# A two-layer decoder: the last mixture of experts on tokens sorted by expert, its routing spread over the next batch

## Chip, cores and metric

The kernel runs on one core of a Trainium2 chip. The time is the device time in microseconds (us) of one execution, inputs and outputs in the chip's memory; what stands below is the median of several runs, and the lowest and highest beside it. One further execution was taken by the profiler.

## What is computed

Four sequences of 512 tokens with 128 features pass two decoder layers. The first has an attention (A), a cross attention (B) and a mixture of 8 experts (C); the second an attention with relative positions (D), a cross attention to 154 context tokens (E), a causal attention with 16 heads (F), and a mixture of experts (G). The change concerns G, which is this, on all 2048 tokens at once:

```python
logits = xf @ router_w + router_b
vals, idx = top_k(logits, 2)
scores = softmax(vals)
cap = int(floor(n * 0.125))                         # 256 of 2048
oh = one_hot(idx, 8)
pos = cumsum(cumsum(oh, axis=0), axis=1)            # over tokens, then over the two choices
emask = oh * (pos < cap)
tmask = sum(emask, axis=-1)
m = max(einsum('tke,e->tk', emask, arange(8)), axis=-1)   # the one expert of a token
def ff(w1e, w2e, w3e):                              # 128 -> 256 -> 128
    return gelu(xf @ w2e * (xf @ w1e)) @ w3e
y = vmap(ff)(w1, w2, w3)[m, arange(n)]
slot = where(tmask[..., None] > 0, y[:, None, :], xf[:, None, :])
out = einsum('tkD,tk->tD', slot, scores)            # added to the residual
```

Each token needs the output of one expert only, `m`, and how many tokens came before it decides which, so the count runs on from batch to batch.

## The kernel before

Tokens lie in tiles of 128, four to a batch (`NT`). Every engine has a program of its own, written out stage by stage, with semaphores between them: `pe_` for TensorE (PE), `act_` for ScalarE, `dve_` for VectorE (DVE), `pool_` for GpSimd (POOL), `sp_` for the queue that issues DMAs. The order of the calls in these programs is the order of the work on that engine; an engine waits where its program waits. `ch(...)` in VectorE's program is a chain: the next instruction waits until this one has ended.

The first layer is written out batch by batch. Its mixture C runs once for all batches on sorted tokens. `dve_C_choose` finds each token's expert, `pe_C_rank` (L666 to L671) and `dve_C_slot` (L679 to L689) give it a row in a buffer in memory, `pool_C_send` (L696) scatters the tokens there by four indirect DMAs a batch. After the last batch a table says for each of 23 tiles (`NS`, 16 tiles and 7 for experts' unfilled ends) which rows and which expert it has (L762 to L780). Then a loop over the 23 tiles, six of them loaded ahead (`NXB`): `flip` transposes one (L709), `hidden` multiplies it with the first weights, which POOL has copied into place (L718, L833), ScalarE does the Gelu (L753), `result` multiplies with the second weights (L729), L798 puts the output into SBUF and the queue stores it to the same rows. Sixteen gathers (L837) bring the rows back in the tokens' order.

The second layer is a hardware loop over the batches (`Fori`), on every engine: the projection of D (`pe_D1`: context of E, bias L320, projection L315), E (`pe_X` and its partners), F, and G. Where the loop turns, VectorE adds the residual (L327) and normalizes it (`dve_norm`), and PE transposes the result (L263) as soon as that is there; until then it runs matmuls without a use (L259). In E the row maxima (L565) follow the scores (L450), and the reciprocals (L575) follow the last of the values (L493). In F the key projections (L1344) are rotated by VectorE (L1489 to L1491), the queries by VectorE (L1501) and added by POOL (L1543).

G before is in `pe_G`, `act_G` and `dve_G`. It is dense: for each of the 8 experts all 512 tokens of the batch go through both hidden matmuls (L1569, L1573, two chunks of 128 features each), ScalarE copies one product out (L1612), VectorE multiplies the two (L1644), ScalarE does the Gelu (L1626), PE multiplies with the third weights (L1599), and VectorE adds what belongs to the expert under a mask (L1700):

```python
ins = V.scalar_tensor_tensor(o, ps[:, 6 + e % 2, i * P:(i + 1) * P],
                             sel[:, i, e:e + 1], x[:, i, :], ALU.mult, ALU.add)
```

The router lies inside this work: gate matmuls (L1560), logits (L1649), the two choices (L611 to L618, twice), the counting matmuls (L1582 to L1587), and the pick of expert and scale (L1659 to L1690). In each turn PE goes on to the next batch only after the last expert.

## Time and profile before

| what | before |
|---|---|
| median of 3 runs | 1775.34 us (1773.99 to 1780.18) |
| profiled execution | 1777.35 us, its span 1775.5 us |
| TensorE (PE) busy | 1538.5 us, 87% |
| VectorE (DVE) busy | 1028.7 us, 58% |
| ScalarE (ACT) busy | 822.4 us, 46% |
| GpSimd (POOL) busy | 192.6 us, 11% |
| mean granted TensorE clock | 0.94 of full |
| share of the chain that ended last | PE 75%, DVE 12%, issue 6%, ACT 2%, SPq 2% |

The span reaches from the first to the last instruction; the time of the execution holds a little more. Busy time of PE counts matmuls of float32, which appear as two records each, and also matmuls without a use. "Issue" in the chain is time in which the engine waited for nothing that the profile shows. The stages lie, in us from the span's start: A and B to 310, C to about 405, D to about 897, and then the loop over E, F and G, with a turn at about 1115, 1333 and 1557.

### The profile page before, as it was taken

What the parts mean: (1) busy time and instruction counts of PE and PEld (TensorE: products, weight loads), DVE (VectorE), ACT (ScalarE), POOL (GpSimd) and SP (SyncE); (2) the same over time, 40 slices, a digit from 0 to 9 for tenths busy, and PEclk for the clock granted to TensorE, in tenths of its full rate; (3) what the DMA queues carried; (4) which work ended last, traced back from release to release, by engine and by line L of the source; (5) the groups of instructions that cost most, each with busy time, mean ns of one, the idle gap of its engine ahead of it and who ended that gap; (6) DMA issues with size and microseconds to landing.
All of it is one profiled execution on the core that took longest, in us unless ns stands there. A gap on an engine that the chain in (4) does not pass through costs nothing.

```text
span 1775.5 us, 46299 instructions
## 1 busy us (share of the span) xinstructions
PE 1538.5 (87%) x18075; PEld 936.6 (53%) x18110; DVE 1028.7 (58%) x2616; ACT 822.4 (46%) x2030; POOL 192.6 (11%) x147
## 2 busy tenths in 40 slices
PE   3988888666399999999779999889998899988998
PEld 2343443663267666666433665346663466534665
DVE  4364553326477777777535765467653666547655
ACT  1313223331266666666422774327643276442764
POOL 1010110234120020200002000020000200002000
PEclk9989989787699999999879999999998999999999
DMA  9500000112230100000030000000000000000000
GB/s 332 226 16 1 16 7 1 40 50 85 60 131 4 35 8 23 19 13 5 16 98 1 2 2 1 12 1 2 2 1 11 1 2 2 1 8 1 2 2 6
DMA packets 54165, 55.25 MB, mean 31 GB/s; under 512 B 26673, under 2 KB 39857, under 8 KB 52785
## 3 DMA queue, kind: packets, MB, share of 16 engines
q1 hardware_dynamic: 52912, 50.05, 8.8%
q8 instruction: 150, 2.46, 0.6%
q0 software_dynamic: 1024, 2.10, 0.4%
q14 instruction: 79, 0.64, 0.1%
HBM read 30.18 MB, written 21.95 MB: 29 GB/s over the span
## 4 chain that ended last, share of the span: by engine, by line
PE 75%; DVE 12%; issue 6%; ACT 2%; SPq 2%; DMA 1%; POOL 0%; ACTq 0%; DVEq 0%; POOLq 0%
PE ps L1002 7%; PE ps L1374 5%; PE ps L1393 5%; PE ps L493 4%; PE ps L982 4%; PE ps L1407 4%; PE ps L992 4%; PE ps L1020 4%; PE ps L1599 3%; PE ps L259 3%; PE ps L1362 3%; DVE arena L565 3%; PE ps L1573 3%; PE ps L1569 3%; PE ps L467 3%
## 5 line engine op out<-in xcount | busy, mean ns | idle before, releaser
L1132 DVE TENSOR_REDUCE nmax<-ps 128x1 f32<-128x512 f32 x256 | 166.8, 684 | 60.7 <-PE ps L992 59.9
L1450 ACT ACTIVATE arena<-ps,arena 128x512 f32<-128x512 f32 (+3 forms) x256 | 135.4, 531 | 117.5 <-DVE arena L1508 109.8
L1508 DVE TENSOR_REDUCE arena<-ps 128x1 f32<-128x512 f32 (+3 forms) x256 | 124.3, 487 | 76.2 <-PE ps L1378 74.1
L1092 ACT ACTIVATE arena<-ps,nmax 128x512 f32<-128x512 f32 x172 | 119.0, 692 | 85.4 <-DVE nmax L1132 84.4
L1393 PE MATMUL ps<-sqc,arena 128*128 128x128 f32 x640 | 108.1, 288 | 20.5 <-DVE arena L1516 19.5
L565 DVE TENSOR_REDUCE arena<-ps 128x8 f32<-128x1232 f32 x64 | 89.2, 1438 | 40.6 <-PE ps L455 40.1
L1140 DVE COPY arena<-ps 128x512 f32<-128x512 f32 x128 | 88.0, 688 | 36.9 <-PE ps L1002 35.4
L575 DVE RECIPROCAL arena<-ps 128x128 f32<-128x128 f32 x8 | 7.7, 959 | 170.0 <-PE ps L493 170.0
L1516 DVE TENSOR_SCALAR arena<-arena 128x512 f32<-128x512 f32 (+3 forms) x256 | 100.8, 394 | 9.1
L1374 PE MATMUL ps<-arena 64*128 64x384 f32 (+3 forms) x512 | 105.2, 489 | 0.0
L259 PE MATMUL ps<-sel,identb 128*128 128x512 bf16 x385 | 100.9, 417 | 3.3 <-issue 2.6
L1407 PE MATMUL ps<-arena 128*64 128x128 f32 x1280 | 98.2, 284 | 0.0
L1002 PE MATMUL ps<-sqc,arena 128*128 128x128 f32 x688 | 95.6, 282 | 2.9 <-issue 1.7
L1461 ACT COPY arena<-ps 128x512 f32<-128x512 f32 (+3 forms) x256 | 96.1, 430 | 3.1 <-PE ps L1393 3.0
L1393 PEld LDWEIGHTS ps<-sqc,arena 128*128 128x128 f32 x640 | 71.4, 141 | 48.5 <-DVE arena L1516 31.4
L1002 PEld LDWEIGHTS ps<-sqc,arena 128*128 128x128 f32 x688 | 74.8, 143 | 22.3 <-issue 17.4
L306 ACT ACTIVATE root<-var 128x4 f32<-128x4 f32 x32 | 6.6, 206 | 158.8 <-DVE var L288 138.5
L1100 ACT COPY arena<-ps 128x512 f32<-128x512 f32 x128 | 74.4, 581 | 11.6 <-PE ps L1002 11.5
L1644 DVE TENSOR_TENSOR arena<-ps,arena 128x512 f32<-128x512 f32 x64 | 43.9, 691 | 58.6 <-PE ps L1573 46.5
L992 PEld LDWEIGHTS ps<-rk,cw 64*128 64x128 f32 x512 | 44.4, 192 | 60.7 <-issue 56.0
L595 POOL TENSOR_TENSOR arena<-arena,m 128x640 f32<-128x640 f32 x8 | 10.0, 1255 | 612.2 <-ACT arena L526 612.2
L992 PE MATMUL ps<-rk,cw 64*128 64x168 f32 (+25 forms) x512 | 75.3, 414 | 0.0
(332 smaller groups left out, 3062.2 us busy)
## 6 DMA issues: line engine op xcount, KB each, us to landing
xs_d<-onehot SPq DMA_DIRECT2D x3, 3072.0 KB, 31.1
cw<-in_cw SPq DMA_DIRECT2D x2, 2048.0 KB, 13.0
rv<-in_rv SPq DMA_DIRECT2D x2, 1536.0 KB, 19.4
late<-in_gw SPq DMA_DIRECT2D x3, 1024.0 KB, 10.5
xs_d<-onehot SPq DMA_DIRECT2D x1, 2560.0 KB, 22.5
onehot<-q_s SPq DMA_DIRECT2D x96, 8.0 KB
arena<-xs_d SPq DMA_DIRECT2D x23, 64.0 KB, 1.8
xs_d<-arena SPq DMA_DIRECT2D x23, 64.0 KB, 1.6
```

The lines of the kernel that those rows point to most:

```text
L259: nc.tensor.matmul(ps[:, FILL[k][1], :], identb[:, :], sel[:, 0:4, :].rearrange("p a n -> p (a n)"), start=True, stop=True)
L565: nc.vector.tensor_reduce(top_x[:, i, :, 2 * hp:2 * hp + 2], ps[:, bank:bank + NG4, 0:2 * KP].rearrange("p g (h k) -> p g h k", h=2)[:, :, ...
L992: nc.tensor.matmul(ps[:, (4 * Q + j) % 5, k0:k1], AI[b % 2][64 * z:64 * z + 64, par * NW + w, :], rk[64 * z:64 * z + 64, r0:r0 + k1 - k0], ...
L1002: ins = nc.tensor.transpose(ps[:, TB[j % 2], i * P:(i + 1) * P], PB[k % 6][:, i * P:(i + 1) * P], c["ident"])
L1092: nc.scalar.activation(PB[k % 6], ps[:, k % 5, :], ACT.Exp, bias=nmax[:, u:u + 1], accum_out=rsum[:, b % 2, u:u + 1]).then_inc(SD["exp"], 1)
L1132: nc.vector.tensor_reduce(nmax[:, k % NU:k % NU + 1], ps[:, k % 5, :], AX.X, ALU.max, negate=True)\
L1374: nc.tensor.matmul(ps[:, FSB[n % 2][h], 0:wd], TF["q%d" % a][HALVES[h], i * P:(i + 1) * P], TF["kr%d" % (a % 2)][HALVES[h], 0:wd], start=T ...
L1393: ins = nc.tensor.transpose(ps[:, FTB[h], j * P:(j + 1) * P], TF["p%d" % (n % 2)][:, h * S + j * P:h * S + (j + 1) * P], c["ident"])
L1407: ins = nc.tensor.matmul(ps[HALVES[h], 4, i * P:(i + 1) * P], TF["v"][:, v0:v0 + KD], PTF[n % 2][h][:, j * P:(j + 1) * P], start=(j == 0), ...
L1450: nc.scalar.activation(TF["p%d" % (n % 2)][:, h * S:h * S + wd], ps[:, FSB[n % 2][h], 0:wd], ACT.Exp, bias=TF["nmax"][:, k4:k4 + 1], accum ...
L1508: nc.vector.tensor_reduce(TF["nmax"][:, k4:k4 + 1], ps[:, FSB[n % 2][h], 0:wd], AX.X, ALU.max, negate=True)\
L1516: nc.vector.tensor_scalar(TF["p%d" % (n % 2)][:, h * S:h * S + wd], TF["p%d" % (n % 2)][:, h * S:h * S + wd], TF["rinv"][:, k4], None, ALU ...
```

## The change

G works on sorted tokens as C does, and its parts move. The loop over the batches is written out on every engine. After F of a batch only the gate and the two choices follow (`pe_G_gate`, `dve_G_gate`). The rest of the routing of batch b stands in the next batch: the counting matmuls ahead of the scores of E, the copy of their result ahead of the first row maximum, the second score's exponential in `act_X`, the pick of the expert ahead of the reciprocals, the ranking matmuls behind the values, the slot in F behind its second norm, the four scatters on POOL ahead of F's rotary additions. After the last batch its routing runs too, then the table, the loop over 23 tiles and 16 gathers. In this loop a tile takes eight hidden records, four result records and one transpose, one ScalarE copy, one product, one Gelu and one copy out of PSUM. POOL copies both hidden weights of the expert together. B and E share their semaphores, so every wait in E counts on from B (`both`); table building is shared between C and G (`dve_tiles`).

```diff
--- before.py
+++ after.py
@@ pe_X
+            if k == "E" and b:
+                pe_G_count(pe, b - 1)
             for n in range(NXH):
+                if k == "E" and b and n == 1:
+                    pe.wait_ge(SG["seen"], b)
                 scores(n)
...
                 values(j)
+            if k == "E" and b:
+                pe_G_rank(pe, b - 1)
             pe_bias(DH[k][0], 1, k + "_bo")
@@ act_X
+            if k == "E" and b:
+                act_G_second(act, b - 1)
@@ dve_X
             dve_norm(dve, ch, b, k, src=y)
+            if k == "E" and b:
+                dve_G_seen(dve, b - 1)
...
             nc.vector.tensor_tensor(low, top_x, high, ALU.subtract).then_inc(s["mt"], 1)
+            if k == "E" and b:
+                dve_G_pick(dve, ch, b - 1)
+            dve.wait_ge(s["pv"], both(k, b) * NPER + NPER)
@@ pe_F
+            if b:
+                pe.wait_ge(SG["slot"], b)
             for i in range(NT):
                 ins = nc.tensor.matmul(ps[:, 5 + i // 2, i % 2 * 256:i % 2 * 256 + 256], xnT[:, i * P:(i + 1) * P],
                                        fwv[:, :], start=True, stop=True)
@@ dve_F
             dve_rms(dve, ch, b, 2, xn[:, :, :], yn, row["F_g1"])
+            if b:
+                dve_G_slot(dve, ch, b - 1)
@@ G
+        def act_G_second(act, b):
+            act.wait_ge(SG["d"], b + 1)
+            nc.scalar.activation(gs["e2"][:, :], gs["t1"][:, :], ACT.Exp).then_inc(SG["e2"], 1)
...
+        def pe_G_rank(pe, b):
+            pe.wait_ge(SG["pick"], b + 1)
+            if b:
+                pe.wait_ge(SG["slot"], b)
...
+        def pool_G_send(pool, b):
+            pool.wait_ge(SG["slot"], b + 1)
+            for n in range(NT):
+                nc.gpsimd.indirect_dma_start(xs_d, bass.IndirectOffsetOnAxis(ap=slot4[:, b * NT + n:b * NT + n + 1], axis=0),
+                                             yn4(b)[:, n, :], None).then_inc(SC["sent"], 16)
+
+        def pe_G(pe):
+            pe.wait_ge(SG["slot"], B)
+            nc.tensor.matmul(ps[:, 0, 0:E2], c["ones"], carry[:, :], start=True, stop=True).then_inc(SG["count"], 1)
+            pe.wait_ge(SG["table"], 1)
...
+            def hidden(s):
+                e = nc.tensor.value_load(expert4[0:1, s:s + 1], min_val=0, max_val=E2 - 1)
+                pe.wait_ge(SC["w1"], NS + s + 1)
+                pe.wait_ge(SC["xt"], NS + s + 1)
+                if s >= 2:
+                    pe.wait_ge(SG["p"], s - 1)
+                for j in range(2 * NC2):
+                    ins = nc.tensor.matmul(ps[:, 2 + j // NC2 + 2 * (s % 2), j % NC2 * P:j % NC2 * P + P],
+                                           TG[f"w{s % 2}"][:, j * P:(j + 1) * P], TG[f"xT{s % 2}"], start=True, stop=True)
+                ins.then_inc(SC["h"], 1)
+                return e
+
+            def result(s, e):
+                pe.wait_ge(SC["hs"], NS * NC1 + s + 1)
+                if s >= 2:
+                    pe.wait_ge(SC["yb"], NS + s - 1)
+                for j in range(NC2):
+                    ins = nc.tensor.matmul(ps[:, 6 + s % 2, 0:P], TG[f"h{s % 2}"][:, j * P:(j + 1) * P],
+                                           gw3[:, bass.ds(e * NC2 + j, 1), :].rearrange("p o n -> p (o n)"),
+                                           start=(j == 0), stop=(j == NC2 - 1))
+                ins.then_inc(SC["y"], 1)
+
+            flip(0)
+            flip(1)
+            e = hidden(0)
+            for s in range(NS):
+                if s + 2 < NS:
+                    flip(s + 2)
+                following = hidden(s + 1) if s + 1 < NS else None
+                result(s, e)
+                e = following
+
+        def act_G(act):
+            nc.scalar.activation(warm[:, 19:20], c["ones"][:, 0:1], ACT.Gelu)
+
+            def linear(s):
+                act.wait_ge(SC["h"], NS + s + 1)
+                if s >= 2:
+                    act.wait_ge(SG["p"], s - 1)
+                nc.scalar.copy(TG[f"a{s % 2}"], ps[:, 3 + 2 * (s % 2), 0:HID2]).then_inc(SG["a"], 1)
+
+            linear(0)
+            for s in range(NS):
+                if s + 1 < NS:
+                    linear(s + 1)
+                act.wait_ge(SG["p"], s + 1)
+                if s >= 2:
+                    act.wait_ge(SC["y"], NS + s - 1)
+                nc.scalar.activation(TG[f"h{s % 2}"], TG[f"p{s % 2}"], ACT.Gelu).then_inc(SC["hs"], 1)
+
+        def dve_G(dve, ch):
...
+            def product(s):
+                dve.wait_ge(SC["h"], NS + s + 1)
+                if s >= 2:
+                    dve.wait_ge(SC["hs"], NS * NC1 + s - 1)
+                dve.wait_ge(SG["a"], s + 1)
+                V.tensor_tensor(TG[f"p{s % 2}"], ps[:, 2 + 2 * (s % 2), 0:HID2], TG[f"a{s % 2}"], ALU.mult).then_inc(SG["p"], 1)
...
+            for s in range(NS):
+                if s + 2 < NS:
+                    copy(s + 2)
+                if s + 1 < NS:
+                    product(s + 1)
+                dve.wait_ge(SC["y"], NS + s + 1)
+                if s >= 4:
+                    dve.wait_ge(SC_st[s % 4], 16 * (st_c[s % 4] + s // 4))
+                V.tensor_copy(TG[f"y{s % 4}"], ps[:, 6 + s % 2, 0:P]).then_inc(SC["yb"], 1)
+            for b in range(B):
+                dve.wait_ge(SC_yg[b], 2 * 16 * NT)
...
+            for z in range(4):
+                pool.wait_ge(SC_st[z], 16 * 2 * st_c[z])
+            for n in range(NTT):
+                nc.gpsimd.indirect_dma_start(yg4(n // NT)[:, n % NT, :], None, xs_d,
+                                             bass.IndirectOffsetOnAxis(ap=slot4[:, n:n + 1], axis=0)).then_inc(SC_yg[n // NT], 16)
@@ the program of TensorE
-            with pe.Fori(0, B) as b:
+            for b in range(B):
                 pe_D1(pe, b)
...
+                pe_X(pe, b, "E")
+                pe_F(pe, b)
+                pe_G_gate(pe, b)
+            pe_G_count(pe, B - 1)
+            pe_G_rank(pe, B - 1)
+            pe_G(pe)
@@ the program of GpSimd
+            for b in range(B):
                 pool_D1(pool, b)
...
+                pool_X(pool, b, "E")
+                if b:
+                    pool_G_send(pool, b - 1)
+                pool_F(pool, b)
+            pool_G_send(pool, B - 1)
+            pool_G(pool)
```

## Rows read from the trace of the kernel before

**Rows 1.** the chain of waits, 1140 to the end: start, us, what

```profile
1285.46 1.06 PE ps L1560 x8
...
1306.91 1.78 PE ps L1599 x16
...
1340.23 1.11 PE ps L263 x4
...
1725.68 1.06 PE ps L1560 x8
```

**Rows 2.** timeline, VectorE at the end: start, us, what [idle before]

```profile
1771.69 1.13 DVE L1700 SCALAR_TENSOR_TENSOR rv<-ps,gt_sel,x 128x128 f32 x4 [0.73 <-PE ps L1599]
```

**Rows 3.** timeline, the turn from the second batch to the third

```profile
1333.32 0.53 PE L426 MATMUL ps<-ctxT,sqw 128*128 128x160 f32 x2 [1.96 <-issue]
...
1335.79 0.82 DVE L552 TENSOR_TENSOR arena<-ps,rowb 128x640 f32<-128x640 f32 x1 [3.20 <-PE ps L429]
...
1335.95 1.16 PE L315 MATMUL ps<-sqw,aoT 128*128 128x128 f32 x8
...
1337.27 0.76 DVE L327 TENSOR_TENSOR x<-ps,rv 128x256 f32<-128x256 f32 x2 [0.65 <-PE ps L315]
```

**Rows 4.** timeline, the router inside G, second batch

```profile
1290.70 0.18 DVE L1649 TENSOR_TENSOR gt_logit<-ps,rowb 128x32 f32<-128x32 f32 x1
...
1293.24 0.19 DVE L618 TENSOR_TENSOR arena<-gt_eq,gs_top 128x32 f32<-128x32 f32 x1
...
1293.98 0.79 PE L1587 MATMUL ps<-arena,sqc 128*128 128x48 f32 x6
...
1297.20 0.16 DVE L1659 TENSOR_SCALAR gs_t<-gs_e 128x4 f32<-128x4 f32 x1
...
1300.33 0.16 DVE L1687 TENSOR_TENSOR gs_cz<-gs_m 128x4 f32<-128x4 f32 x1
```

**Rows 5.** timeline, VectorE at the end of cross attention

```profile
1379.99 0.96 DVE L575 RECIPROCAL arena<-ps 128x128 f32<-128x128 f32 x1 [22.79 <-PE ps L493]
```

**Rows 6.** timeline, first layer, from the last choice to the first tile

```profile
317.41 0.41 PE L666 MATMUL ps<-oh,sqc 128*128 128x32 f32 x2 [1.47 <-DVE oh L618]
...
319.69 0.17 DVE L689 CAST slot<-gs_top 128x4 int32<-128x4 f32 x1
...
327.30 6.32 SPq L816 DMA_DIRECT2D arena<-xs_d  x6
...
329.28 0.45 PE L709 MATMUL ps<-sqc,arena 128*128 128x128 f32 x1 [8.77 <-DMA arena<-xs_d]
```

**Rows 7.** timeline, first layer, from the last tile through the gathers

```profile
383.53 0.29 DVE L798 TENSOR_TENSOR arena<-ps,arena 128x128 f32<-128x128 f32 x1 [1.41 <-PE ps L729]
...
387.25 1.00 POOL L837 DMA_INDIRECT late<-xs_d,slot  x1 [9.53 <-DMA xs_d<-arena]
...
406.21 0.94 POOL L837 DMA_INDIRECT late<-xs_d,slot  x1 [0.30 <-issue]
```

**Rows 8.** timeline of POOL, first rotary addition of the third batch

```profile
1401.19 1.27 POOL L1543 TENSOR_TENSOR arena<-arena 128x512 f32<-128x512 f32 x1 [62.95 <-DVE arena L1501]
```

**Rows 9.** timeline, first layer's tile loop, first hidden and last transpose

```profile
331.16 2.05 PE L718 MATMUL ps<-arena 128*128 128x128 f32 x8 [0.49 <-DVE arena L787]
...
377.66 0.27 PE L709 MATMUL ps<-sqc,arena 128*128 128x128 f32 x1
```

**Rows 10.** groups by form, ScalarE: what, count, busy us, mean ns, idle before

```profile
L1461 ACT COPY arena<-ps 128x256 f32<-128x256 f32 x64 | 20.7, 374 | 2.5 <-PE ps L1393 2.5
...
L1626 ACT ACTIVATE arena<-arena 128x512 f32<-128x512 f32 x64 | 40.4, 631 | 13.1 <-DVE arena L1644 13.1
```

**Rows 11.** DMA issues of the page: tiles, op, count, us to landing

```profile
late<-xs_d,slot POOLq DMA_INDIRECT x16, 2.5
```

**Rows 12.** windows: stretch, us, busy of each engine, PE clock, DMA share

```profile
360.00:365.00 5.00, 3.29 (x19) 2.94 (x19) 0.58 (x2) 1.57 (x7) 0.92 (x2) 0.79 0.24 66
...
1341.00:1345.00 4.00, 2.46 (x14) 0.98 (x14) 0.00 (x0) 1.38 (x3) 0.00 (x0) 1.00 0.00 0
```

More of the change, by code:

```diff
@@ L445, in scores @@
                 if n >= 2:
-                    pe.wait_ge(s["top"], b * NXH + n - 1)
+                    pe.wait_ge(s["top"], both(k, b) * NXH + n - 1)
                 k0 = 0 if k == "B" else min(i * P, KS)
@@ L1544, in pool_F @@
                     .then_inc(SF["qr"], 1)
-        SG = {n: sem("s_g_" + n) for n in ("gate", "d", "e2", "oh", "cum", "h", "a", "p", "hs", "y", "acc")}
+        SG = {n: sem("s_g_" + n) for n in ("gate", "d", "e2", "oh", "cum", "seen", "pick", "rank", "slot", "count", "table", "a", "p")}
+        ld_c, st_c = ([len(range(z, NS, n)) for z in range(n)] for n in (NXB, 4))
+        NC2 = HID2 // P
         used[0] = 0
-        TG = dict(**{n + str(i): cut(S) for n in ("a", "p") for i in range(2)}, h0=cut(2 * S), h1=cut(2 * S),
-                  oh=cut(NT * 2 * E2), sum=cut(2 * E2))
@@ L1629, in dve_G, with dve_G_seen, dve_G_pick @@
-        def dve_G(dve, ch, b):
+        def dve_G_seen(dve, b):
+            dve.wait_ge(SG["cum"], b + 1)
+            nc.vector.tensor_copy(TG["cum"], ps[:, 7, 64:64 + NT * CE]).then_inc(SG["seen"], 1)
+        def dve_G_pick(dve, ch, b):
             V = nc.vector
-            dve_rms(dve, ch, b, 3, xn[:, :, :], yn, row["F_g2"])
-            ch(nc.vector.tensor_tensor(x[:, :, :], x[:, :, :], xn[:, :, :], ALU.add))
-            dve.wait_ge(SG["gate"], b + 1)
-            lg, oh1, oh2, pos, junk, sel = (gt[n][:, :, :] for n in ("logit", "oh1", "oh2", "pos", "junk", "sel"))
+            lg, oh1, oh2, pos, junk = (gt[n][:, :, :] for n in ("logit", "oh1", "oh2", "pos", "junk"))
@@ new lines, in dve_G, with copy @@
+        def dve_G(dve, ch):
+            V = nc.vector
+            dve.wait_ge(SG["count"], 1)
+            dve_tiles(ch, SG["table"])
+            def copy(s):
+                dve.wait_ge(SC["tx"], NS + s + 1)
+                if s >= 2:
+                    dve.wait_ge(SC["h"], NS + s - 1)
+                V.tensor_copy(TG[f"xT{s % 2}"], ps[:, s % 2, 0:P]).then_inc(SC["xt"], 1)
+            def product(s):
+                dve.wait_ge(SC["h"], NS + s + 1)
+                if s >= 2:
+                    dve.wait_ge(SC["hs"], NS * NC1 + s - 1)
+                dve.wait_ge(SG["a"], s + 1)
+                V.tensor_tensor(TG[f"p{s % 2}"], ps[:, 2 + 2 * (s % 2), 0:HID2], TG[f"a{s % 2}"], ALU.mult).then_inc(SG["p"], 1)
+            copy(0)
+            copy(1)
+            product(0)
+            for s in range(NS):
[9 more added lines that the diff above has]
+                dve.wait_ge(SC_yg[b], 2 * 16 * NT)
+                for i in range(NT):
+                    ins = V.scalar_tensor_tensor(xo4(b)[:, i, :], yg4(b)[:, i, :], cy4[:, b * NT + i:b * NT + i + 1], xo4(b)[:, i, :],
+                                                 ALU.mult, ALU.add)
+                ins.then_inc(s_xout, 1)
@@ new lines, in sp_G, with load @@
+        def sp_G(sp):
+            sp.wait_ge(SC["sent"], 2 * 16 * NTT)
+            sp.wait_ge(SG["table"], 1)
+            def load(s):
+                r = sp.value_load(rows4[0:1, s:s + 1], min_val=0, max_val=XROWS - P)
+                if s >= NXB:
+                    sp.wait_ge(SC["tx"], NS + s - NXB + 1)
+                sp.dma_start(XBG[s % NXB], xs_d[bass.ds(r, P), :]).then_inc(SC_ld[s % NXB], 16)
+            for s in range(NXB):
+                load(s)
+            for s in range(NS):
+                r = sp.value_load(rows4[0:1, s:s + 1], min_val=0, max_val=XROWS - P)
+                sp.wait_ge(SC["yb"], NS + s + 1)
+                sp.dma_start(xs_d[bass.ds(r, P), :], TG[f"y{s % 4}"]).then_inc(SC_st[s % 4], 16)
+                if s + NXB < NS:
+                    load(s + NXB)
@@ L1919, in _ @@
             dve.wait_ge(s_const[4], 16 * (len(GROUPS[4]) + 1))
-            ch = Chain(dve, SH[1]["ch"], CH[last])
-            with dve.Fori(0, B) as b:
-                ch.turn(b)
+            ch = Chain(dve, SH[1]["ch"], 0)
+            ch.turn(0)
+            for b in range(B):
                 dve_D1(dve, ch, b)
-                if "E" in stages:
-                    dve_X(dve, ch, b, "E")
-                if "F" in stages:
-                    dve_F(dve, ch, b)
-                if "G" in stages:
-                    dve_G(dve, ch, b)
-                if last != "G":
-                    nc.vector.tensor_copy(tmp[:, 0:1], x[:, 0, 0:1]).then_inc(s_xout, 1)
-                ch.end()
+                dve_X(dve, ch, b, "E")
+                dve_F(dve, ch, b)
+                dve_G_gate(dve, ch, b)
+            dve_G_seen(dve, B - 1)
+            dve_G_pick(dve, ch, B - 1)
+            dve_G_slot(dve, ch, B - 1)
+            dve_G(dve, ch)
         @block.gpsimd
```

267 lines of the change are left out of this document (119 added, 148 removed).

## Prediction, made before the changed kernel ran

> **What bounds the kernel now.** I read the chain of waits first, over the second layer only, to see which engine carries it, then the timeline at one turn of the batch loop, then the same views over the first layer's mixture of experts, which already runs on sorted tokens and so has rows for nearly everything that the change adds.
>
> The second layer is a loop over four batches, and the tensor engine (PE) carries it: the chain in there is made of pieces such as 16 expert matmuls in 1.78 us, 0.111 us each [rows 1]. In each turn the last mixture (G) runs all 8 experts over all 512 tokens. The stretch from the start of the gate's matmuls (L1560) to the first transpose of the next batch's cross attention (L263) holds the rest of G, the loop's turn, and the next batch's residual and norm. In the second turn it is 1285.46 to 1340.23, 54.77 us [rows 1]; the other two turns repeat the pattern with 54.85 and 56.16, together 165.8. After the last gate, which starts at 1725.68, the kernel has 49.8 us left to its end at 1775.5 [rows 1, 2]. What the change gains and pays lies in these four stretches, and in what it inserts into cross attention (E) and attention (F).
>
> **Part 1, the three turns between batches.** The dense experts and the turn of the loop go. Between gate and transpose there stays: the gate's matmuls, 1.06, so they end at 1286.5. PE goes on with context, bias and projection, which last from 1333.32 to 1337.11, 3.8 us, so to 1290.3 [rows 3]. DVE takes the logits through both top choices, L1649 at 1290.70 to the end of the last L618 at 1293.43, 2.73 us [rows 4], now from 1286.65 to 1289.4; then L552, 0.82, to 1290.3; then residual and norm, 2.96 from L327 (1337.27) to L263 (1340.23) [rows 1, 3]. The two engines come to the residual together, so this chain has no slack. The transposes start at about 1293.4, 7.9 us after the gate's start; three turns cost 23.8 where 165.8 stood: minus 142.0.
>
> **Part 2, what is inserted in the next batch.** The counting matmuls stand ahead of the first scores, where PE has just waited for q_t, and nothing covers them: L618 ends at 1293.43 and L1587 at 1294.77, 1.3 us [rows 4], three times: plus 3.9. PE's wait on "seen" comes behind the first scores, which cover DVE's copy of 64 columns. Who waits there is DVE's row of maxima, and it is late by the same 1.3, not more. The pick goes where DVE sits idle for 22.79 us ahead of L575 [rows 5]: L1659 at 1297.20 to L1687 at 1300.33, with one step more and one copy less 3.3 us [rows 4], and four updates of x: hidden, and 4.5 a turn if it weren't. The ranking matmuls stand behind the values, while PE waits for those reciprocals: nothing, at most their 1.3. The slot chain runs in F before L1489, where DVE waits for the key projections: nothing, at most its 1.0; ranking and slot together are 2.45 (L666 at 317.41 to the end of L689 at 319.86 [rows 6]). PE's wait on the slot comes after the key projections, when the slot has long been there. On POOL four sends stand ahead of the rotary additions. I price a send by the pace of layer 0's gathers, 15 steps from 387.25 to 406.21, 1.26 each [rows 7], 5.0 in all. They start at about 1393.7 and end at 1398.8; POOL's first addition now starts at 1401.19 [rows 8], so the margin is 2.4 us. Behind POOL stand DVE's rotation of the third pair and then PE's queries.
>
> **Part 3, the new tail**, on the clock of the old kernel. The last gate ends at 1726.74. Choice with its handover 2.85, to 1729.6; counting 1.35; copy 0.3; the pick up to the one-hot 3.3, to 1734.6 (ScalarE's exponential is ready before); ranking and slot 2.45, and 0.4 because PE has been idle, to 1737.5. From the slot (319.86) to the first transposed tile (329.28) layer 0 takes 9.42, for count, table, four sends and the load [rows 6]: first tile at 1746.9.
>
> **The tile loop** has no counterpart and is put together from neighbours. PE's order is transpose, hidden(s+1), result(s). Layer 0's tile has 17 records, 1.89 us at 0.111, and PE sets its pace; over the whole loop it took 2.20 a tile (329.28 to 377.66 in 22 steps, with its stalls) [rows 6, 9]. Here a tile has 1 + 8 + 4 = 13 records, 1.44 us, but ScalarE copies tile s+1 before it does the Gelu of tile s, so PE must wait. Hidden to its end 1.06 (eight records and the way through the array, as the gate's x8 [rows 1]); a handover of 0.15; the copy of 256 columns, 0.374, of which 0.34 until the next can start; the Gelu of 256, which lies between this 0.374 and the 0.631 of 512 columns and which I take at 0.42, nearer the copy [rows 10]; 0.15; result and transpose, 5 x 0.111; and 0.09 for a weight load after a wait. That is 2.75 us a tile; the bounds are 1.89 and the 4.31 of rival 1. The first hidden starts 1.88 after the first transpose (329.28 to 331.16), the second 1.0 later, 21 tiles are 57.8, the last takes 3.8 to its output: 64.5. The first hidden of layer 0 lasted 2.05 instead of 1.06 [rows 9], the clock being at 1.2 GHz after the idle time; I add 3.5 for such a start. So 68 us, to 1814.9.
>
> **The flush.** From the last output tile (L798 ends at 383.82) to the first gather 3.43; 18.96 to the start of the sixteenth [rows 7]; 2.5 to land [rows 11]; four additions and a handover 1.25, as L1700's 1.13; and from DVE's last end (1772.82) to the end of the span 2.7 [rows 2]. Together 28.8: 1843.7, 68.2 later than the old end. With minus 142.0 and plus 3.9 the span ends at 1705.6, 69.9 below 1775.5. The profiled execution took 1777.35 by its own clock, so 1707.4; the median of the runs, 1775.34, lies 2.0 lower and gives 1705.4. **I say 1706.**
>
> **Rivals.** (1) *The tensor clock falls in the tile loop.* At 1.2 GHz hidden takes 2.05 and a record twice 0.111: 2.05 + 0.15 + 0.34 + 0.42 + 0.15 + 1.11 + 0.09 = 4.31 a tile; 21 x 1.56 = 33 more, less most of the 3.5 already counted: 1736. For it: PE would be busy for about 61% of the loop, and in 360 to 365 a single wait left it 3.29 of 5 us and a clock of 0.79, where 1.00 is 2.4 GHz. Against it: 1341 to 1345 had 2.46 of 4 us busy at 1.00 [rows 12]; and a tile at 1.2 GHz would be 76% busy, which may lift the clock by itself.
>
> The Trainium skill, "TensorE: Matmul & The Clock Gate", section "HAM oscillation — how this bites in real kernels", tells of a kernel in which every group of matmuls starts throttled because a wait lies before it. If each tile here behaved so, rival 1 would hold from end to end; the row of 1341 to 1345 speaks against it.
>
> (2) *The loop keeps nearer to PE's own pace*: at layer 0's 2.2 a tile 12 us less, 1694; at 1.89, 1687. (3) *The routing isn't covered, and the change fails at what it says*: pick 4.5, ranking and slot 2.45 and sends 5.0 would then stand in each batch, 12 x 3 = 36: 1742. Against it: each lies beside a longer wait. (4) *Slower than before*: a tile becomes one serial chain at the lower clock that includes its load. Transpose 0.6, copy 0.45, hidden 2.2, copy 0.55, product 0.45, Gelu 0.55, result 1.1 make 5.9, and a load 2.0 (L816 at 327.30 to L709 [rows 6]): 7.9 x 23 = 182 in place of 68, so 1820. It decides from 5.9 us a tile (2.75 + 70 / 22). Against it: six load buffers, while layer 0 with as many kept 2.20.
>
> **How the numbers follow.** Forecast 0.58, with its own range 1698 to 1716 (the period by 0.3 either way, 7 us, and stretches at the lower clock in cross attention that move from turn to turn, 3 us). Rival 1 0.20, rival 2 0.12, rival 3 0.06, rival 4 0.03, the rest between. The range 1692 to 1738 takes in rival 1 and the nearer half of rival 2, and leaves out some 0.15. About 0.3% is what a measurement can tell from no change; only rival 4 and 0.02 around it lie there or above: faster 0.95, same 0.02, slower 0.03.
>
> **What would show it.** The gate to the next L263 at 8 us instead of 55; counting matmuls 1.3 us directly ahead of the first scores; the pick inside a stretch of DVE that still ends with the values; POOL's first rotary addition as long after F's transposes as now; 20 us from the last gate to the first tile; tiles 2.7 to 2.8 us apart at a clock of 1.00; 29 us from the last tile to the end. The prediction is wrong first if the loop's clock reads 0.50, or if anything but hidden, copy, Gelu, result sets the period.

## The result, and the profile after

The changed kernel takes 1721.14 us (median of 4 runs, 1717.45 to 1723.11) where the one before took 1777.76 beside it: 0.968 of it (95% interval 0.964 to 0.971), 57 us less where 70 were forecast. The median lies in the stated range of 1692 to 1738, and 5 us above the forecast's own, 1698 to 1716. A second set of five runs gave 1720.09 and 0.968 (0.966 to 0.970). The profiled execution took 1719.98, its span is 1718.2.

The page of the changed kernel: its span, the busy time of the engines, and the granted clock in 40 slices.

```profile
span 1718.2 us, 43781 instructions
...
PE 1428.4 (83%) x17646; PEld 877.7 (51%) x17681; DVE 983.7 (57%) x2543; ACT 747.1 (43%) x1928; POOL 237.5 (14%) x202
...
PEclk9999999796699999999978999899989998999796
```

The turn from the second batch to the third, PE's timeline (start us, us, engine, line, operation, [idle before]); it answers to [rows 1, 3]:

```profile
1240.02 1.06 PE L1591 MATMUL ps<-gwr,xnT 128*128 128x8 f32 x8 [0.68 <-ACT xnT L269]
1240.93 0.52 PE L429 MATMUL ps<-ctxT,sqw 128*128 128x160 f32 x2
...
1248.29 1.10 PE L262 MATMUL ps<-sqc,xn 128*128 128x128 f32 x4 [0.56 <-DVE xn L291]
1250.06 1.13 PE L438 MATMUL ps<-xnT,sqw 128*128 128x512 f32 x2 [0.67 <-ACT xnT L269]
1252.01 0.41 PE L1624 MATMUL ps<-g_oh,sqc 128*128 128x64 f32 x2 [0.82 <-issue]
1252.25 0.39 PE L1625 MATMUL ps<-ohsum,sqc 128*128 128x64 f32 x2
1252.47 0.79 PE L1629 MATMUL ps<-g_oh,sqc 128*128 128x48 f32 x6
1253.19 1.35 PE L453 MATMUL ps<-arena,q_t 32*128 32x320 f32 x8
1254.48 1.21 PE L458 MATMUL ps<-xmask,identb 128*128 128x308 bf16 x4
```

From the gate to the next transposes it is 8.27 us where [rows 1] have 54.77, and the same to 0.01 in all three turns. Behind the q projection (L438) come the counting matmuls (L1624 to L1629), 1.2 us ahead of the first scores (L453). And there is something that the forecast's sum doesn't have: the first scores take 1.35 us for eight and the mask's matmuls (L458) 1.21 for four. In the kernel before (PE's timeline, second batch of the second layer) these were 0.82 and 0.70:

```profile
1125.72 0.82 PE L450 MATMUL ps<-arena,q_t 32*128 32x320 f32 x8 [0.87 <-ACT q_t L535]
1126.47 0.70 PE L455 MATMUL ps<-xmask,identb 128*128 128x308 bf16 x4
```

The clock has fallen, from its level of 2.4 GHz to that of 1.2. The windows show it for that batch, the changed kernel first and then the kernel before (stretch, us, busy of PE, PEld, DVE, ACT, POOL, granted clock, DMA share, GB/s):

```profile
1071.10:1075.10 4.00, 2.48 (x9) 1.14 (x9) 0.74 (x3) 2.24 (x5) 0.00 (x0) 1.00 0.00 0
1075.10:1079.10 4.00, 4.00 (x26) 2.39 (x29) 0.56 (x2) 0.00 (x0) 0.00 (x0) 0.59 0.00 0
```

```profile
1121.95:1125.70 3.75, 2.22 (x6) 0.86 (x7) 0.71 (x3) 2.13 (x4) 0.00 (x0) 1.00 0.00 0
1125.70:1129.70 4.00, 3.83 (x36) 1.73 (x36) 2.50 (x2) 0.00 (x0) 0.00 (x0) 1.00 0.00 0
```

The tail of the changed kernel, PE's timeline, from the last gate to the first tile:

```profile
1594.50 1.06 PE L1591 MATMUL ps<-gwr,xnT 128*128 128x8 f32 x8 [0.67 <-ACT xnT L269]
1598.44 0.69 PE L1624 MATMUL ps<-g_oh,sqc 128*128 128x64 f32 x2 [2.89 <-DVE g_oh L633]
...
1604.16 0.64 PE L1683 MATMUL ps<-oh,sqc 128*128 128x32 f32 x2 [3.41 <-DVE oh L1670]
...
1616.96 0.45 PE L1723 MATMUL ps<-sqc,arena 128*128 128x128 f32 x1 [8.69 <-DMA arena<-xs_d]
```

One tile of its loop, from the timeline of all engines:

```profile
1643.04 1.13 PE L1732 MATMUL ps<-arena 128*128 128x128 f32 x8 [0.23 <-issue]
...
1644.20 0.37 ACT L1764 COPY arena<-ps 128x256 f32<-128x256 f32 x1 [2.37 <-PE ps L1732]
...
1644.47 0.42 ACT L1773 ACTIVATE arena<-arena 128x256 f32<-128x256 f32 x1
...
1645.05 0.71 PE L1742 MATMUL ps<-late,arena 128*128 x4 [0.88 <-ACT arena L1773]
...
1645.60 0.27 PE L1723 MATMUL ps<-sqc,arena 128*128 128x128 f32 x1
```

A tile is hidden (1643.04), copy (1644.20), Gelu (1644.47), result (1645.05), transpose (1645.60), next hidden (1646.11): 3.07 us. And the loop's clock, the third number from the right, in the windows of the same kernel:

```profile
1617.00:1622.00 5.00, 4.13 (x17) 3.57 (x18) 1.21 (x4) 0.37 (x1) 0.61 (x1) 0.50 0.23 65
1622.00:1690.00 68.00, 42.66 (x284) 33.88 (x282) 19.99 (x65) 15.55 (x45) 12.27 (x20) 1.00 0.13 38
```

In the repeat of the same kernel (run 9) the clock stood at the lower level for 9 us more of the loop, and the second, third and fourth period took 4.03, 4.02 and 3.85 us:

```profile
1613.65:1627.60 13.95, 11.16 (x45) 9.69 (x45) 3.07 (x10) 1.92 (x6) 1.88 (x4) 0.50 0.13 38
1627.60:1688.60 61.00, 38.25 (x254) 30.45 (x254) 18.12 (x59) 14.01 (x41) 11.06 (x18) 1.00 0.14 39
```

The whole account, in us, from the timelines of three profiles. "Again" is the repeat. The first row is code that the change doesn't touch, and the forecast took it from the kernel before:

| stretch | forecast | changed | again |
|---|---|---|---|
| start to the second layer's first context matmul | 891.2 | 882.0 | 889.5 |
| to the first gate | 175.9 | 180.8 | 175.9 |
| three turns, gate to transposes | 23.8 | 24.8 | 24.8 |
| transposes to first scores, three batches | 15.2 | 15.1 | 15.2 |
| first scores to DVE's reciprocals, three | 101.6 | 114.1 | 110.7 |
| reciprocals to the gate, three | 379.9 | 377.7 | 375.1 |
| last gate to the first tile's transpose | 21.2 | 22.5 | 22.5 |
| to the last tile's output | 68.0 | 72.9 | 75.0 |
| to the end | 28.8 | 28.3 | 28.3 |
| span | 1705.6 | 1718.2 | 1717.0 |

Two rows hold most of what the changed kernel took beyond the sum: from the first scores to the reciprocals (+9 to +12.5), and the tile loop (+5 to +7). The first row moves by itself: over thirteen profiles with the same code in it, it lay between 882.0 and 891.2.

### The profile page after: what moved, and what is told of

It reads as the page before. It is cut to its first block, busy times and chain, and to the rows that moved or that the text cites. A ratio compares the mean times of both kernels' runs of the same rounds, so it can differ in the third digit from the quotient of the medians.

```text
span 1718.2 us, 43781 instructions
## 1 busy us (share of the span) xinstructions
PE 1428.4 (83%) x17646; PEld 877.7 (51%) x17681; DVE 983.7 (57%) x2543; ACT 747.1 (43%) x1928; POOL 237.5 (14%) x202
## 4 chain that ended last, share of the span: by engine, by line
PE 71%; DVE 16%; issue 4%; ACT 3%; DMA 2%; POOL 2%; SPq 2%; ACTq 0%; POOLq 0%; DVEq 0%
PE ps L1022 7%; PE ps L1396 6%; PE ps L496 5%; PE ps L1415 5%; PE ps L1002 4%; PE ps L1429 4%; PE ps L1012 4%; DVE arena L578 4%; PE ps L1040 4%; PE ps L258 3%; PE ps L1384 3%; PE ps L470 3%; PE ps L1054 2%; PE ps L1438 2%; PE ps L1732 2%
## 5 line engine op out<-in xcount | busy, mean ns | idle before, releaser
L1472 ACT ACTIVATE arena<-ps,arena 128x512 f32<-128x512 f32 (+3 forms) x256 | 135.3, 531 | 119.3 <-DVE arena L1532 112.9
L1429 PEld LDWEIGHTS ps<-arena 128*64 128x64 f32 x1280 | 68.8, 138 | 13.6 <-issue 1.7
L258 PEld LDWEIGHTS ps<-sel,identb 128*128 128x128 bf16 x408 | 44.6, 109 | 53.3 <-issue 19.2
## 6 DMA issues: line engine op xcount, KB each, us to landing
cw<-in_cw SPq DMA_DIRECT2D x2, 2048.0 KB, 12.2
```

The costliest lines, as they stand in the source:

```text
L258: nc.tensor.matmul(ps[:, FILL[k][1], :], identb[:, :], sel[:, 0:4, :].rearrange("p a n -> p (a n)"), start=True, stop=True)
L1429: ins = nc.tensor.matmul(ps[HALVES[h], 4, i * P:(i + 1) * P], TF["v"][:, v0:v0 + KD], PTF[n % 2][h][:, j * P:(j + 1) * P], start=(j == 0), ...
L1472: nc.scalar.activation(TF["p%d" % (n % 2)][:, h * S:h * S + wd], ps[:, FSB[n % 2][h], 0:wd], ACT.Exp, bias=TF["nmax"][:, k4:k4 + 1], accum ...
```

## The experiments

Three questions: what the loop's turn was worth by itself and whether the routing is really hidden; why the clock falls at the scores; what sets 3.07 us a tile. Changes against the changed kernel (0.968 of the kernel before) are given by the ratios, 0.001 being 1.8 us; these ratios carry about 0.005 either way, so the stretches of the trace decide where the ratios don't.

**1. The loop written out, alone.** In each of four engines, in the kernel before:

```diff
-            with pe.Fori(0, B) as b:
+            for b in range(B):
```

> The kernel before with its second loop over the batches written out, four batches one after another in the program, and nothing else of the change. Theory: the loop's turn is a small part of the 142 us that go from the three turns between batches; in the trace of before, PE waits some 2.0 us at each turn for nothing that the profile shows, so the kernel should be 6 us shorter than the one before, at most 9, and the stretch from the gate's matmuls to the next cross attention's first transpose should read 53 in place of 55 us. Rival: the turn lies beside DVE's additions and is hidden, and the time is the same within 2 us; or the longer program must be fetched, and it is up to 10 us slower. The run also repeats the cross attention of the kernel before, first scores to reciprocals 32.8, 36.0 and 32.8 us: if it reads 37 to 39 here too, the 12.5 us that the changed kernel takes more there are not the inserted routing's doing.

Measured: 0.994 (0.992 to 0.997), span 1769.1. The three turns took 52.26, 52.26 and 57.26 us where they had 54.85, 54.77 and 56.16. So the turn of the loop is worth 2.5 us, and in the third turn a stretch at the lower clock swallowed it (1500.6 to 1505.0 read 0.55, 1505 to 1510 read 0.71). From scores to reciprocals 32.9, 36.0 and 33.8: as before the change, so the 37 to 39 there don't come from writing out the loop; what of them the inserted count causes, runs 3 and 4 show.

**2. The routing uncovered.** Count, "seen", second, pick, rank and slot behind their own gate:

```diff
                 pe_G_gate(pe, b)
-            pe_G_count(pe, B - 1)
-            pe_G_rank(pe, B - 1)
+                pe_G_count(pe, b)
+                pe_G_rank(pe, b)
```

> The changed kernel with the routing of each batch (count, pick, rank, slot) put right behind its own gate, where nothing covers it, instead of inside the next batch's cross attention; the sends stay where they are. Against the changed kernel. Theory: each of the three batches pays 0.3 for the copy, 1.3 for the count, 3.3 for the pick, 2.45 for rank and slot and some handovers, 8 us, of which the 1.3 for the count were paid already: 3 x 7 = 21 us slower, 1742, and the turn from the gate to the next transpose reads 15 to 16 us in place of 8.2. If the routing inside cross attention is what pulls the clock down there, the stretch from the first scores to the reciprocals goes back from 37.7, 37.3 and 39.1 to 33 to 36 us, which gives back up to 12: then only 10 us slower. Rival: the clock in there goes its own way, and the stretch stays at 37 or more, or changes in both directions from batch to batch; then 21 us or more.

Measured: 0.983 (0.978 to 0.988), 27 us more than the changed kernel. From the gate to the first scores it was 25.3, 27.0 and 27.1 us where it had been 13.2 to 13.5, 13.2 a batch: more than the 7 expected, for two reasons that the timeline shows. From the gate's end to PE's next context matmul it is 10.3 to 10.8 us, because the choice (2.9) is now uncovered too, which had lain beside context and projection; and PE comes out of it at the lower clock, so that context, bias and projection take 7 us in place of 3.8.

```profile
1253.00:1257.00 4.00, 2.31 (x10) 2.21 (x10) 1.45 (x10) 0.00 (x0) 0.00 (x0) 0.50 0.00 0
...
1261.00:1265.00 4.00, 4.00 (x15) 3.12 (x14) 1.73 (x6) 1.88 (x3) 1.39 (x2) 0.50 0.03 8
```

In return the clock was back before the scores, and scores to reciprocals read 32.5 us in all three batches: part of the loss came back there, as the first theory said. So the cover is real, and worth 27 us.

**3. The counting matmuls ahead of the transposes**, in place of six fills:

```diff
+            if k == "E" and b:
+                pe_G_count(pe, b - 1)
             pe_transpose(pe, b, k)
...
-            if k == "E" and b:
-                pe_G_count(pe, b - 1)
             for n in range(NXH):
```

> The changed kernel with the counting matmuls moved from ahead of the first scores to ahead of the transposes of the next cross attention, where PE does useless fills now (six of the fills are left out for them). Against the changed kernel. Theory 1: the 1.3 us of the count ahead of the scores go in each of three batches, minus 4, and as the counting matmuls with the wait in front of them are what lets the clock fall just there, the first scores run at the clock that they had in the kernel before and the stretch from scores to reciprocals falls from 38 to 33 to 36 us: together minus 10 to minus 16. Theory 2: the clock falls wherever its own rhythm puts it, and only the 4 us go: 1717, with the stretch still at 37 or more in some batches.

Measured: 0.962 (0.957 to 0.967), 11 us less than the changed kernel. From transposes to scores 3.8 us again instead of 5.0, and the block of first scores (64 matmuls and the mask's 16) took 10.6 us in each batch. From scores to reciprocals it was 35.5, 35.1 and 32.6 us, within the 33 to 36 expected.

**4. Fills behind the q projection**, count left where it is:

```diff
+            if k == "E" and b:
+                for _ in range(4):
+                    nc.tensor.matmul(ps[:, 7, :], identb[:, :], sel[:, 0:4, :].rearrange("p a n -> p (a n)"), start=True, stop=True)
             mask = bmask if k == "B" else xmask
```

> The changed kernel with four useless matmuls (128x512 bf16, about 0.85 us together) put behind the q projection of the cross attention in the three batches that carry routing, where PE waits 0.8 us for q_t ahead of the counting matmuls and the first scores. The counting matmuls stay where they are. Against the changed kernel, whose eight 64-record blocks of first scores took 13.2, 12.2 and 13.0 us there. Theory: the clock falls at the scores because the stretch ahead of them, with the wait and the small counting matmuls in it, leaves PE nearly idle; filled, it holds the clock: the block reads 10.5 to 11.2 in all three batches as it did with the count moved away (10.5, 10.6, 10.5), and the kernel is 6 to 10 us shorter. Rival: it is the counting matmuls behind q_t themselves, or their 1.3 us of delay, that matter, and fills ahead of them change nothing: 12 to 13.5 in the block, the same time within 3 us.

Measured: 0.960 (0.955 to 0.966), 14 us less, blocks of 11.2, 10.6 and 10.6 us, and 32.9, 32.6 and 32.6 us from scores to reciprocals. One such block here (third batch) as a window, and behind it one of the changed kernel (second batch); the column behind POOL's is the clock:

```profile
1253.80:1264.50 10.70, 8.23 (x82) 3.48 (x81) 9.37 (x8) 0.00 (x0) 0.00 (x0) 1.00 0.00 0
```

```profile
1076.00:1089.50 13.50, 11.12 (x81) 4.45 (x81) 9.70 (x8) 0.00 (x0) 0.00 (x0) 0.75 0.00 0
```

Runs 3 and 4 change different things, the place of the count and the wait ahead of it, and both bring the clock back. All profiles together, the block of first scores in the three batches concerned:

| kernels | blocks, us |
|---|---|
| count behind the wait for q_t, not filled (changed kernel twice, runs 5, 6, 7) | 11.5 to 13.6, 15 of 15 |
| nothing inserted there (before, run 1) | 10.6 to 11.2, 6 of 6 |
| count moved away or the wait filled (runs 2, 3, 4, 8, 10, 11) | 10.6 to 11.2, 18 of 18 |

The block is only a part of the stretch from scores to reciprocals. Split there, as the sum of the three batches in each profile, it reads:

| kernels | blocks, us | behind them, us |
|---|---|---|
| before, run 1 | 33.6, 33.0 | 68.0, 69.7 |
| count behind the wait (changed kernel, run 9, runs 5, 6, 7) | 38.3, 37.8, 38.4, 39.2, 37.2 | 75.8, 72.9, 68.6, 68.8, 69.6 |
| count moved away (runs 3, 8, 10, 11) | 31.7 each | 71.4, 73.0, 73.0, 72.8 |
| wait filled (run 4), routing uncovered (run 2) | 32.4, 31.7 | 65.8, 65.9 |

The count's price is in the first column: 38.2 on average for 33.6. In the second the clock falls too, with the count and without it (here the changed kernel, and then run 3, each in the second batch), and there the changed kernel's first profile is the longest of all, for no reason that a run shows:

```profile
1092.90:1099.70 6.80, 6.80 (x36) 3.02 (x36) 2.68 (x18) 4.57 (x8) 0.00 (x0) 0.50 0.00 0
```

```profile
1097.50:1104.30 6.80, 6.80 (x32) 2.22 (x28) 1.78 (x10) 4.32 (x8) 0.00 (x0) 0.50 0.00 0
```

The Trainium skill ("TensorE: Matmul & The Clock Gate", section "HAM oscillation — how this bites in real kernels") tells of groups of matmuls that each start throttled because a wait of 3 to 5 us for a DMA lies before them. Here the clock fell with a wait of 0.82 us ahead of ten small matmuls (the two waits before it were 0.56 and 0.67), so a short wait is no safeguard; the same wait alone, 0.87 us in the kernel before, did not do it. And in the changed kernel's tile loop, with 0.88 us of waiting in every tile, the clock stayed at 1.00 once it had risen.

**5. The Gelu of tile s ahead of the copy of tile s+1:**

```diff
-                if s + 1 < NS:
-                    linear(s + 1)
                 act.wait_ge(SG["p"], s + 1)
...
                 nc.scalar.activation(TG[f"h{s % 2}"], TG[f"p{s % 2}"], ACT.Gelu).then_inc(SC["hs"], 1)
+                if s + 1 < NS:
+                    linear(s + 1)
```

> The changed kernel with ScalarE's order in the tile loop turned round: the Gelu of tile s comes before the copy of tile s+1, so that hidden, copy, Gelu, result is no longer one chain. Against the changed kernel. Theory: this chain sets the period of 3.07 us, and without it the period falls to what the next engine needs, PE's own 1.9 to 2.2 us (DVE and GpSimd have under 1.9 in the trace): 22 x 0.9 to 1.1, 20 to 25 us less, 1697 to 1701. Rival: something that the loop's trace shows only as idle (PE's register load of the expert ahead of hidden, 0.24 us in each tile, or the wait for the output buffers) sets it, and the period stays at 2.7 or more: at most 8 us less.

Measured: 0.950 (0.944 to 0.955), 33 us less by the ratios, 20 in the loop itself (first to last hidden 48.6 us for 68.5); another 7 us lie between scores and reciprocals, which the edit doesn't touch. The mean period fell to 2.16 us. The chain hidden, copy, Gelu, result was the bound. But the period was not even, mostly 1.73 to 2.3 and up to 2.89, and in the longest tiles PE now waited for loads (0.57 and 0.39 us ahead of two transposes).

**6. PE's register load of the expert behind hidden:**

```diff
-                e = nc.tensor.value_load(expert4[0:1, s:s + 1], min_val=0, max_val=E2 - 1)
                 pe.wait_ge(SC["w1"], NS + s + 1)
...
                 if s + 1 < NS:
                     hidden(s + 1)
+                    following = which(s + 1)
                 result(s, e)
```

> The changed kernel with PE's register load of the tile's expert moved from ahead of hidden(s+1) to behind it, ahead of the result's wait for the Gelu. Nothing else. Against the changed kernel. Theory: the 0.24 us of idle time that the trace puts between transpose and hidden in each tile, with no releaser, is this load, and it lies in the chain hidden, copy, Gelu, result, transpose: the period falls from 3.07 to about 2.8 and the kernel is 5 to 6 us shorter; the prediction's sum for the tile of 2.75 then lacked only this. Rival: the gap is the handover of hidden's own waits, and stays: period 3.05 or more, same time within 2 us. The cross attention is that of the changed kernel, so the run also repeats its score blocks: if the clock falls by chance there, some of the three will read 10.5 to 11.2.

Measured: 0.961 (0.956 to 0.966), 13 us less; the period is 2.59 us, 0.48 less, twice what was expected:

```profile
1643.00 0.71 PE L1743 MATMUL ps<-late,arena 128*128 x4 [0.88 <-ACT arena L1778]
1643.54 0.27 PE L1723 MATMUL ps<-sqc,arena 128*128 128x128 f32 x1
1643.65 1.06 PE L1734 MATMUL ps<-arena 128*128 128x128 f32 x8
```

Hidden starts 0.11 us behind the transpose, where it had been 0.51, and lasts 1.06 for 1.13. Only 0.23 of the 0.48 had shown as "issue"; for the rest, hidden now starts 0.16 ahead of the transpose's modelled end and is 0.07 shorter. The Trainium skill ("Runtime: NRT & Kernel Launch", section "Instruction fetch mechanics") has about 0.2 us a register for the loads that the runtime adds; here a load of the kernel's own, from SBUF, cost 0.48. This run, run 3 and run 9 also show tiles at the clock of 0.50: among their first periods are two to three of 4.02 us, where rival 1 had 4.31.

**7. Fills ahead of the tile loop:**

```diff
+            for _ in range(24):
+                nc.tensor.matmul(ps[:, 7, :], identb[:, :], sel[:, 0:4, :].rearrange("p a n -> p (a n)"), start=True, stop=True)
             pe.wait_ge(SG["table"], 1)
```

> The changed kernel with 24 useless matmuls (128x512 bf16) behind the counting matmul of the last routing, where PE waits some 9 us for the table and the first tile. Against the changed kernel. Theory: the tile loop begins at the lower clock because PE has been nearly idle since the last gate (0.50 from 1598 to 1622); with the fill the clock is back at 1.00 before the first transpose, the first hidden lasts 1.1 instead of about 2.1, and the loop is 2.5 to 3.5 us shorter. Rival: the fills run over the arrival of the first tile by as much as they bring, and the time is the same within 1.5 us. The run repeats cross attention and the loop's period of the changed kernel, 3.07.

Measured: 0.967 (0.961 to 0.973), no difference; loop 68.3 us for 68.5.

```profile
1594.43 6.95 PE L1718 MATMUL ps<-sel,identb 128*128 128x512 bf16 x24
1603.24 0.30 PE L1725 MATMUL ps<-sqc,arena 128*128 128x128 f32 x1 [1.86 <-DMA arena<-xs_d]
1604.25 0.33 PE L1725 MATMUL ps<-sqc,arena 128*128 128x128 f32 x1 [0.71 <-DMA arena<-xs_d]
1605.01 2.04 PE L1734 MATMUL ps<-arena 128*128 128x128 f32 x8 [0.43 <-DVE arena L1786]
```

Neither side of the expectation held. The fills raised the clock, ended 1.86 us early because of it, and over the three waits that follow it fell again: the first hidden still lasted 2.04.

**8. Edits 3, 5, 6 and 7 together.**

> The changed kernel with four edits together: the counting matmuls ahead of the transposes in place of fills, the Gelu of tile s ahead of the copy of tile s+1, the register load behind hidden, and the 24 fills ahead of the tile loop. Against the changed kernel. Theory: the first gives 10, the second 22 to 28 as it did alone, the register load nothing more, because with the new order of ScalarE PE waits for the Gelu anyway and the load lies beside that wait; the last 3: together 35 to 41 less, 1680 to 1686. Rival: the register load still lies in the new chain, and gives its 5 us here too: 1675 to 1680; or the faster loop starves on its loads, and the gains don't add: above 1690.

Measured: 1690.09 us, 0.948 (0.943 to 0.953), 36 us less than the changed kernel, which is not distinguishable from run 5's 33. The first six periods were 1.55 to 1.74 us, PE's own pace; then they were mostly 2.05 to 2.44, with one of 4.47, in which PE waited 2.70 us for a load. The reason for the 2.2 stands on SyncE's queue:

```profile
1617.61 0.36 SPq L1834 DMA_DIRECT2D xs_d<-arena  x1
1618.73 0.34 SPq L1827 DMA_DIRECT2D arena<-xs_d  x1
1619.82 0.36 SPq L1834 DMA_DIRECT2D xs_d<-arena  x1
1620.94 0.40 SPq L1827 DMA_DIRECT2D arena<-xs_d  x1
```

A store and a load in 2.2 us, without a wait: SyncE issues as fast as it can, and six loads were ahead only at the start.

**9. The changed kernel again,** beside the next two.

> The changed kernel once more, beside the next two on the same chip, as their reference and to see how far its profile repeats. Theory: the score blocks of the three batches that carry routing read 11.5 to 13.6, never 11.2 or less, and the tile loop's period 3.05 to 3.09 at a clock of 1.00; the stages ahead of the second layer, whose code is the old one, end anywhere from 882 to 891 us at the first context row of cross attention. Rival: a block of 11.2 or less appears here too, and then the clock's fall is only likelier with the inserted count, not bound to it.

Measured: 1720.09 us, 0.968 (0.966 to 0.970); blocks of 12.9, 12.7 and 12.2 us, period mostly 3.05 to 3.15, first context row at 889.5. The theory held for the blocks and the first context row. For the loop it held from about the fifth period on; the slow ones ahead of that, at the lower clock, it had not foreseen. The account is the last column above.

**10. Row numbers kept in registers,** in the kernel of run 8:

```diff
-                r = sp.value_load(rows4[0:1, s:s + 1], min_val=0, max_val=XROWS - P)
+                r = kept.pop(s)
                 sp.wait_ge(SC["yb"], NS + s + 1)
```

> The kernel with the four edits, and SyncE keeps each tile's row number in its register from the load to the store of the same tile, instead of reading it a second time. Against the kernel with the four edits, whose first tiles came 1.55 to 1.74 us apart while six loads were ahead, and the later ones 2.1 to 2.3, with SyncE issuing a store and a load in every 2.2 us without a wait. Theory: SyncE's two register reads and two issues are the bound there, 1.1 us for each pair; without one of the reads its turn is about 1.5 to 1.6, PE's own 1.6 to 1.7 becomes the period, and the loop is 8 to 12 us shorter: 1679 to 1682. Rival: the issue itself costs the 1.1 us, or the tiles wait for the transfers (1.8 us to landing) and not for their issue: the period stays above 2.0, the time within 3 us.

Measured: 1681.87 us, 0.946 (0.943 to 0.949). The periods alternate between 1.55 and 1.74 nearly to the end, the loop went from 47.0 to 39.7 us, and SyncE's queue has slack:

```profile
1620.89 0.34 SPq L1829 DMA_DIRECT2D arena<-xs_d  x1
1621.33 0.38 SPq L1836 DMA_DIRECT2D xs_d<-arena  x1
1622.46 0.33 SPq L1829 DMA_DIRECT2D arena<-xs_d  x1
```

From load to store it is 0.44 us where it had been 1.09: the register load was 0.65 of it. The loop is now bound by PE, 1.65 a tile, where 13 matmuls of 0.111 make 1.44. The whole kernel gained less than the loop by the ratios, within what they can tell.

**11. Fills in both places besides.** Run 10 with four fills behind the q projection (into another PSUM bank than in run 4) and 32 ahead of the loop.

> The kernel of the run before with two more edits: the four useless matmuls behind the q projection of cross attention, on another bank, and 32 instead of 24 fills ahead of the tile loop, so that they end when the first tile lands (24 ended 1.86 us early, and the clock had fallen again by the first hidden, which lasted 2.0). Against that kernel. Theory: the fills in cross attention take the stretch from scores to reciprocals from about 35 to 32.6 in each batch, as they did alone, minus 5 to 8; the longer fill holds the clock through the first tile, minus 1 to 2: together minus 6 to 10. Rival: with the count already moved the stretch is as good as it gets on average and the fills only shift where the clock falls; the tail's fall comes from the two short waits at the first tiles and stays: within 3 us.

Measured: 1678.13 us, 0.946 (0.943 to 0.948), the same as run 10. Scores to reciprocals together 104.6 us for 104.7: with the count moved away, the fills bring nothing. Run 4, which filled the wait and left the count in place, has 98.2; from the transposes on, count included, it has 112.9 us where runs 3 and 11 have 114.5 and 115.9. So filling the wait was at least as good as moving the count, by one profile of each, and no run joins it to the edits of the loop. The longer fill did work (the first hidden lasted 1.13, and the loop 37.1 us for 39.7). Runs 10 and 11 are the fastest here, some 40 us below the changed kernel.

## Why the prediction was right, and where it was off

**Part 1, the turns: right.** 8.27 us each where the sum had 7.9. It named a chain without slack, and the trace has it; run 1 shows that 2.5 of the 47 us a turn were the loop itself.

**Part 2, what is inserted: right on cover, wrong on one price.** The counting matmuls cost the 1.3 us a batch that they were priced at (transposes to scores 5.0 us for 3.8). Pick, rank and slot are hidden: reciprocals to gate is 375 to 378 us for 380. POOL's sends started at 1127.45, took 1.27 each as priced, and the first rotary addition came 2.71 us after the last, waiting for DVE as before:

```profile
1131.33 0.96 POOL L1711 DMA_INDIRECT xs_d<-rv,slot  x1 [0.30 <-issue]
1134.99 1.26 POOL L1567 TENSOR_TENSOR arena<-arena 128x512 f32<-128x512 f32 x1 [2.71 <-DVE arena L1525]
```

Rival 3 is refuted by these and by run 2, which removed the cover and cost 27 us. What failed is the sentence that the row of maxima "is late by the same 1.3, not more". It was late by 1.3 plus what the lower clock took in the scores: 4.6 us over the three batches, 3.6 to 5.6 in the five profiles. The forecast had put 3 us into its own range for stretches "that move from turn to turn". This one did not move, it came in 15 of 15 batches. The other 7.8 us of the first profile's 12.5 lie behind the block of first scores. There the five profiles have 68.6 to 75.8 us and four without the count ahead of the scores 71.4 to 73.0, so that part isn't shown to be the count's: it is of the kind that moves, only larger than 3.

**Part 3, the tail and the tiles: the pieces right, one left out.** 22.5 us from the gate to the first tile for 21.2: the counting matmuls took 2.4 us at the lower clock where 1.35 were taken from a place at the higher. The tile was put together as hidden, copy, Gelu, result, transpose, and this is the chain that run 5 broke; run 6, without the register load, has 2.59 us for the forecast's 2.75. Missing was the register load itself, 0.48 us in each tile. It stood in the code, ahead of hidden, and no row of the kernel before was looked up for it. Together 3.07 for 2.75, 7 us over 21 tiles, of which the generous start took a part; the loop took 72.9 for 68.0, and 75.0 in the repeat, where the lower clock lasted longer. The flush was 28.3 for 28.8.

**The rivals.** Rival 1 is refuted for the loop as a whole, whose clock read 1.00 from 1622 to 1690, but it holds for the loop's start: the clock read 0.50 for the first 5 us of the loop, for 14 in the repeat and for 18 in run 3, with 4.02 us a tile. The forecast's 3.5 us for the start stand for this. Rival 2's 2.2 a tile was not what the change does but what the loop can do: run 5 reached 2.16, and run 10, with the edits together, 1.65. Rival 4 would have needed 5.9 us a tile.

**The sum.** The span missed by 12.6 us: 12.5 from scores to reciprocals (4.7 of them in the blocks), 4.9 in the loop, 1.3 ahead of it, 1.0 in the turns and 4.9 in the first batch, less 9.2 ahead of the second layer, 2.2 from reciprocals to gates, and 0.6 in the two small rows. The 9.2 and the 4.9 are stages that carry no routing; in the repeat they were 1.7 and 0.0. Together they took 4.3 us off the miss, which is luck. What stays open is why the stretch behind the blocks was so long in this profile; over the five profiles the row lies 5.2 to 12.5 above the forecast.

## What to carry to other kernels

Small matmuls that are inserted behind a wait of PE are not priced by their own time: look at the clock of the dense work right behind them, and put them ahead of other small work instead, in the place of fills, or fill the wait ahead of them. In a loop of short tiles, write down every register load of each queue with the waits and the matmuls: here one on PE cost 0.48 us a tile and one on SyncE set the pace once ScalarE's order was mended. And in a chain over several engines, the order of two steps on an engine that is idle three quarters of the time (Gelu before copy) was worth the most of all single edits in the loop, 20 us.

## What the runs showed of the hardware that was not expected

- A register load cost 0.48 us on PE's queue (period 3.07 to 2.59) and 0.65 on SyncE's (1.09 to 0.44 from load to store); an issue with its register load took 1.1 us there.
- The same code ahead of the second layer ended anywhere from 882.0 to 891.2 us over thirteen profiles, as much as one of the terms in question.
- Useless matmuls of 128x512 bf16 started at the lower clock took 6.95 us for 24, and the clock they had raised fell again over three waits of 1.86, 0.71 and 0.43 us (run 7). Without the first of them it held (run 11).
